# Cross attention of a decoder layer: pieces in the middle of a chunk, a ring of four banks for maxima and pieces, three single banks for scores

## The reference

```python
x = x + retention(layernorm(x))                    # 16 heads of 16, group norm over the batch entry
x = x + cross_attention(layernorm(x), ctx)         # ctx: 8 x 1601 x 256
x = x + mixture_of_experts(layernorm(x))           # 8 experts, 2 chosen, plus a shared one
```

```python
q, k, v = x @ Wq.T + bq, ctx @ Wk.T + bk, ctx @ Wv.T + bv
attn = softmax(q @ k.T / 4)                        # 512 queries x 1601 keys
out = (attn @ v) @ Wo.T + bo
```

## Time and profile before

| what | value |
| --- | --- |
| median of three runs | 2397.34 us |
| the profiled execution | 2399.05 us, of which span 2396.9 |
| PE busy | 2174.8 us (91%) |
| DVE busy | 1511.4 us (63%) |
| ACT busy | 1158.0 us (48%) |
| POOL busy | 431.2 us (18%) |
| first score of cross attention, last one | 464.12, 1957.03 |

### The profile page before, as it was taken

The page is one execution under the profiler, slowest core; times in us unless marked ns, Lnnn a source line. Parts: engine busy times, 40 slices in busy tenths (PEclk is TensorE's granted clock), DMA queues, the critical chain, the costliest instruction groups (busy, mean ns, idle before and its releaser), DMA issues. The chain is left out here.

```text
span 2396.9 us, 35042 instructions
## 1 busy us (share of the span) xinstructions
PE 2174.8 (91%) x12914; PEld 1201.8 (50%) x12946; DVE 1511.4 (63%) x2944; ACT 1158.0 (48%) x1521; POOL 431.2 (18%) x470
## 2 busy tenths in 40 slices
PE   6888867599999999999999999999999978899999
PEld 4656544244444444444444434444443337778887
DVE  6888874476676676676667677667668827622221
ACT  2313121156666666666656666666666663222222
POOL 1101021002102112112111210210211005332222
PEclk9999986589999999999989999999999998999999
DMA  4000005504223321520630531422341001000000
GB/s 160 1 0 0 0 4 100 110 1 100 56 56 82 74 56 50 106 56 2 141 69 1 100 95 16 100 55 56 74 81 29 1 16 59 0 9 9 18 18 18
DMA packets 45360, 118.58 MB, mean 49 GB/s; under 512 B 9120, under 2 KB 21408, under 8 KB 45088
## 3 DMA queue, kind: packets, MB, share of 16 engines
q1 hardware_dynamic: 45232, 116.88, 21.9%
HBM read 77.30 MB, written 38.81 MB: 48 GB/s over the span
## 5 line engine op out<-in xcount | busy, mean ns | idle before, releaser
L1142 DVE TENSOR_REDUCE x_mx<-x_ps 128x1 f32<-128x512 f32 x1536 | 956.1, 684 | 400.8 <-PE x_ps L897 400.1
L1050 ACT ACTIVATE x_probs<-x_ps 128x1024 f32<-128x1024 f32 (+1 forms) x832 | 810.2, 1021 | 507.9 <-PE x_ps L956 507.9
L897 PE MATMUL x_ps<-x_kst,x_qst 48*128 48x512 f32 x1536 | 591.4, 467 | 67.9 <-issue 23.9
L897 PEld LDWEIGHTS x_ps<-x_kst,x_qst 48*128 48x128 f32 x1536 | 264.7, 192 | 583.9 <-DVE x_mx L1142 446.4
L956 PE MATMUL x_ps<-x_qst,x_kst 50*128 50x512 f32 (+1 forms) x1664 | 498.3, 432 | 2.5 <-ACT x_probs L1050 2.4
L944 PE MATMUL x_ps<-x_probs,x_vst 128*17 128x512 f32 (+1 forms) x3328 | 449.1, 612 | 6.3 <-ACT x_ou L1034 5.9
L956 PEld LDWEIGHTS x_ps<-x_qst,x_kst 50*128 50x128 f32 (+1 forms) x1664 | 259.3, 185 | 66.4 <-ACT x_probs L1050 49.9
L1569 DVE TENSOR_TENSOR f_hid_whole<-f_ps,f_act_g 128x512 f32<-128x512 f32 x80 | 55.2, 691 | 241.5 <-PE f_ps L1326 232.9
L1441 ACT ACTIVATE f_act_g<-f_ps 128x512 f32<-128x512 f32 x80 | 47.7, 596 | 246.3 <-remote 126.4
L1507 POOL TENSOR_TENSOR f_hid_rest<-f_hid_whole,f_hid_rounded 128x512 fp32r<-128x512 f32 x80 | 103.1, 1289 | 234.0 <-ACT f_hid_rounded L1447 234.0
L1082 POOL TENSOR_TENSOR x_vst<-x_v_all,x_bv 128x768 f32<-128x768 f32 x64 | 66.4, 1069 | 428.0 <-ACT x_v_all L1009 349.4
(11 more groups left out here) (191 smaller groups left out, 2540.6 us busy)
## 6 DMA issues: line engine op xcount, KB each, us to landing
x_kst<-k_parts SPq DMA_DIRECT2D x192, 200.1 KB, 8.6
k_parts<-x_kp SPq DMA_DIRECT2D x16, 1601.0 KB, 6.1
x_ctxT<-in_ctxT SPq DMA_DIRECT2D x8, 1601.0 KB, 7.4
x_qst<-q_parts SPq DMA_DIRECT2D x192, 64.0 KB, 2.4
q_parts<-x_qp SPq DMA_DIRECT2D x8, 1024.0 KB, 4.3
x_all<-in_x SPq DMA_DIRECT2D x8, 512.0 KB, 3.8
out<-x_all SPq DMA_DIRECT2D x8, 512.0 KB, 2.9
x_qst<-x_mrows SPq DMA_DIRECT2D x128, 4.0 KB
```

What stands on the lines that cost most here:

```text
L897: m = pe.matmul(o, qst[mg][rows, pair, t * P:(t + 1) * P], kst[mg][rows, pair, i * 512:(i + 1) * 512], start=True, stop=True)
L1050: nc.scalar.activation(probs[0:w, s % 4, :, :], ps[0:w, 2 * (s % 2):2 * (s % 2) + 2, :], ACT.Exp, scale=HD ** -0.5).then_inc(exp_done, 1)
L1142: nc.vector.tensor_reduce(out=mx[:, 2 * pair + half, t, i:i + 1], in_=o, axis=AX.X, op=ALU.max).then_inc(drained_v, 1)
```

## The change

Five things are done together, all in cross attention.

- The ring for maxima and pieces has four banks (4 to 7) instead of three; the values' bank is 3.
- Scores have three single banks (0 to 2) instead of two double ones. Heads are counted one by one in the order of issue: score i waits for exponential i-3 and increments `s_filled` itself. ACT runs one exponential of 512 columns per head instead of one of 1024 per pair. `probs` keeps its size.
- The piece of a chunk stands between the two halves: maximum, scores of pair 0, maximum, piece, maximum, scores of pair 1, maximum, values. ACT copies it between the exponentials of pair 0 and those of pair 1, and DVE follows the same order.
- In the prologue the k pieces of f = 1 are split by POOL, after it has placed v of group 0 and before groups 1 to 3.
- In the prologue SP loads the shift rows of group 0 after the spill of f = 1 and before it loads groups 2 and 3.

```diff
-W_BANKS = 3
+W_BANKS = 4
+S_BANKS = 3
-    return [[(first[g][c], second[g][c], pieces[g][c]) for c in range(SC)] for g in range(G)]
+    return [[(first[g][c], pieces[g][c], second[g][c]) for c in range(SC)] for g in range(G)]
-        PV, WORK = 4, 5
+        PV, WORK = S_BANKS, S_BANKS + 1
-        probs = sb("x_probs", [P, 4, 2, T])
+        probs = sb("x_probs", [P, 2 * GH, T])
 # SP
-            for f in range(KT):
-                spill_k(0, f)
-                load_group(0, 2 * f)
-                load_group(0, 2 * f + 1)
+            spill_k(0, 0)
+            load_group(0, 0)
+            load_group(0, 1)
+            spill_k(0, 1)
             load_shift(0, done(LEADER, ("shift", 0)))
+            load_group(0, 2)
+            load_group(0, 3)
 # PE
+            def issued(j):
+                return 2 * (j // 2) + (1 - j % 2)
             def scores(b, g, c, pair):
-                n = b * S_ITEMS + g * 2 * SC + 2 * c + pair
                 w = min(P, S - c * P)
-                if n >= 2:
-                    pe.wait_ge(exp_done, n - 1)
                 for h in (1, 0):
+                    n = GH * (b * CHUNKS + g * SC + c) + issued(2 * pair + h)
+                    if n >= S_BANKS:
+                        pe.wait_ge(exp_done, n - S_BANKS + 1)
                     rows = slice(h * ROWS, h * ROWS + XR + MR)
-                    m = pe.matmul(ps[0:w, 2 * (n % 2) + h, :], kst[g][rows, pair, c * P:c * P + w],
-                                  qst[g][rows, pair, :], start=True, stop=True)
-                m.then_inc(s_filled, 1)
+                    pe.matmul(ps[0:w, n % S_BANKS, :], kst[g][rows, pair, c * P:c * P + w],
+                              qst[g][rows, pair, :], start=True, stop=True).then_inc(s_filled, 1)
...
+                        first, pieces, second = PLANS[b][g][c]
+                        n = woven(b, g, c, 0, n, first)
                         for i in range(len(pieces)):
                             fill(b, n + i, g)
-                        n += len(pieces)
+                        n = woven(b, g, c, 1, n + len(pieces), second)
 # ACT
-                            s = b * S_ITEMS + g * 2 * SC + 2 * c + pair
-                            act.wait_ge(s_filled, s + 1)
-                            if s >= 4:
-                                act.wait_ge(pv_used, s // 2 - 1)
-                            nc.scalar.activation(probs[0:w, s % 4, :, :], ps[0:w, 2 * (s % 2):2 * (s % 2) + 2, :],
-                                                 ACT.Exp, scale=HD ** -0.5).then_inc(exp_done, 1)
+                            x = b * CHUNKS + g * SC + c
+                            for s in range(GH * x + 2 * pair, GH * x + 2 * pair + 2):
+                                act.wait_ge(s_filled, s + 1)
+                                if x >= 2:
+                                    act.wait_ge(pv_used, x - 1)
+                                nc.scalar.activation(probs[0:w, s % (2 * GH), :], ps[0:w, s % S_BANKS, :],
+                                                     ACT.Exp, scale=HD ** -0.5).then_inc(exp_done, 1)
 # POOL
-            for g in range(G):
+            place_v(0)
+            for item in k_pieces(1):
+                split_k(pool, nc.gpsimd, 0, item[1], item[2], done(LEADER, item))
+            for g in range(1, G):
                 place_v(g)
 # DVE, prologue
-                elif item[0] == "k":
+                elif item[0] == "k" and item[1] == 0:
```

More of the change, by code:

```diff
@@ L649 @@
 STARTS = [sum(len(items) for items in ITEMS[:n]) for n in range(len(ITEMS))]
-S_ITEMS = 2 * SC * G
+CHUNKS = SC * G
 LEADER, TRAILER = -1, B
@@ L939, in values, with woven @@
                     pe.wait_ge(v_ready, b * 2 * G + 2 * (g + 1))
-                pe.wait_ge(exp_done, b * S_ITEMS + (g * 2 * SC + 2 * (q + 1)))
+                x = b * CHUNKS + g * SC + q
+                pe.wait_ge(exp_done, GH * (x + 1))
                 w = min(P, S - q * P)
                 for j in range(GH):
-                    slot = (g * 2 * SC + 2 * q + j // 2) % 4
+                    slot = (GH * x + issued(j)) % (2 * GH)
                     m = pe.matmul(ps[32 * j:32 * j + HD + 1, PV, :], vst[g][0:w, q, j, :],
-                                  probs[0:w, slot, j % 2, :], start=q == 0, stop=q == SC - 1)
+                                  probs[0:w, slot, :], start=q == 0, stop=q == SC - 1)
                 m.then_inc(pv_used, 1)
+            def issued(j):
+                return 2 * (j // 2) + (1 - j % 2)
             def scores(b, g, c, pair):
-                n = b * S_ITEMS + g * 2 * SC + 2 * c + pair
                 w = min(P, S - c * P)
-                if n >= 2:
-                    pe.wait_ge(exp_done, n - 1)
                 for h in (1, 0):
+                    n = GH * (b * CHUNKS + g * SC + c) + issued(2 * pair + h)
+                    if n >= S_BANKS:
+                        pe.wait_ge(exp_done, n - S_BANKS + 1)
                     rows = slice(h * ROWS, h * ROWS + XR + MR)
-                    m = pe.matmul(ps[0:w, 2 * (n % 2) + h, :], kst[g][rows, pair, c * P:c * P + w],
-                                  qst[g][rows, pair, :], start=True, stop=True)
-                m.then_inc(s_filled, 1)
+                    pe.matmul(ps[0:w, n % S_BANKS, :], kst[g][rows, pair, c * P:c * P + w],
+                              qst[g][rows, pair, :], start=True, stop=True).then_inc(s_filled, 1)
+            def woven(b, g, c, pair, n, some):
+                ahead = len(some) - 1 if some and all(item[0] == "max" for item in some) else 0
+                for i in range(ahead):
+                    fill(b, n + i, g)
+                scores(b, g, c, pair)
+                for i in range(ahead, len(some)):
+                    fill(b, n + i, g)
+                return n + len(some)
             for n in range(len(PROLOGUE)):
@@ L967, in _ @@
                     for c in range(SC):
-                        *woven, pieces = PLANS[b][g][c]
-                        for pair in range(2):
-                            some = woven[pair]
-                            ahead = len(some) - 1 if some and all(item[0] == "max" for item in some) else 0
-                            for i in range(ahead):
-                                fill(b, n + i, g)
-                            scores(b, g, c, pair)
-                            for i in range(ahead, len(some)):
-                                fill(b, n + i, g)
-                            n += len(some)
+                        first, pieces, second = PLANS[b][g][c]
+                        n = woven(b, g, c, 0, n, first)
                         for i in range(len(pieces)):
                             fill(b, n + i, g)
-                        n += len(pieces)
+                        n = woven(b, g, c, 1, n + len(pieces), second)
                         if c:
@@ L1060, in _ @@
                                 evacuate(b * G + g)
-                        for item in [item for part in PLANS[b][g][c] for item in part]:
-                            if item[0] in BY_ACT:
-                                drain(b, n, g)
-                            n += 1
+                            for item in [item for part in PLANS[b][g][c][2 * pair:2 * pair + 2] for item in part]:
+                                if item[0] in BY_ACT:
+                                    drain(b, n, g)
+                                n += 1
             act.wait_ge(drained_v, done(B - 1, ("norm", G - 2)))
@@ L1102, in _ @@
                 if b:
-                    pool.wait_ge(pv_used, b * (S_ITEMS // 2))
+                    pool.wait_ge(pv_used, b * CHUNKS)
                     place_v(G - 1)
```

4 lines of the change are left out of this document (2 added, 2 removed).

## The result

The changed kernel takes 2212.57 us (median of four, 2199.31 to 2222.89) against 2405.89 of the kernel before in the same comparison (2396.11 to 2418.30): a ratio of 0.9191, 95% interval 0.9111 to 0.9271. The forecast, 2245 of 2397.34, was a ratio of 0.936; so the kernel became faster, by about a quarter more than forecast. The profiled execution took 2199.31 (span 2197.5), 199.7 less than the profiled one of before; the forecast for that difference was 152.

The account below looks back on a forecast made before the run. PE and DVE waiting for each other by turns, from too short a ring, were taken as the bound. Savings of 118 + 7 - 7 + 34 = 152 us from 2399 gave 2247, as median 2245 us; range 2195 to 2310.

Parts of the forecast that it names:

- The ring and the place: Chunks with maxima and a piece: four banks, piece in the middle, 3.93 to 3.56 us, 118 us over 319 chunks.
- the switch from pairs to a full-array matmul: On PE, before piece and before values: 0.42 us from start to start; the middle position's two added switches cost 0.30.
- One saving for all pieces: All 319 chunks with maxima and a piece save 0.37 us each, as the piece's length cancels: 118 us.
- none is late: In chunks with the piece in the middle, DVE drains each bank before PE's next maximum or piece needs it.
- The three score banks: Chunks without a piece: fourth score waits for first exponential, period 2.59; 72 chunks save 7 us, last 17 lose 7.
- Exponentials and increments at nothing: Cross attention: exponentials of 512 at 0.50 us each, covered by PE, and 832 more score increments, both priced at 0.
- The prologue: Start of cross attention: POOL's splits and earlier shift rows bring the first score from 464 to 435; start saves 34 us.
- B: Rival: exponentials' round trip replaces the bank wait even with the piece in the middle; period 3.75, about 2312 us; chance 0.12.
- C: Rival: PE's switches cost nothing where weights load ahead; chunk 3.26 us, whole kernel about 2150 us; chance 0.10.
- A: The forecast itself: chunk with a piece 3.56 us, whole kernel 2245 us; chance 0.64.
- D: Rival: another wait stands behind the first, so only the start counts; 2363 to 2385 us; chance 0.08.
- E: Rival: PE's clock falls in 97 chunks without a piece, adding 176 us; about 2421 us, slower; chance 0.06.

Follow-up runs that it names:

- the transposes chunk above: A transposes chunk of the kernel before with only the piece moved to the middle: chunk 3.29 us; that kernel 2277.16 us, ratio 0.947.
- The experiment at the end: The changed kernel with a fourth score bank, one of the ring's, in the last 17 chunks: 2193.42 us, ratio 0.9121.
- the first profile: The first profiled execution of the changed kernel, with nothing further changed: 2199.31 us; a later profiled execution of the same kernel took 2223.96.
- after: The changed kernel, all five parts against the kernel before: 2212.57 us, ratio 0.9191; run once more, 2211.64 us, ratio 0.9185.

## Why the prediction was right, and where its size was off

**The ring and the place: right, and mis-sized.** PE waited for banks, DVE idled while PE did piece and values, and with the piece in the middle no matmul of a full chunk waits: that is what the timeline shows. The term that was mis-sized is the switch from pairs to a full-array matmul. I priced it at 0.42 from the earlier trace rows and used it twice. Measured, the piece starts 0.32 to 0.33 after the second pair and the values 0.33 after the fourth: 0.34 + 0.33 + 1.06 + 0.34 + 0.33 + 0.98 = 3.38. The maximum of the earlier trace rows was no neutral witness: it had just restarted after a wait and ran 0.49, where one in a flow of pairs runs 0.39. The experiments have both: 0.43 after the delayed fourth pair with the piece at the end, 0.43 after the delayed fourth maximum in the transposes chunk above, 0.33 where the pair before flowed. So a stall costs its own length and another 0.1 behind it. A chunk with a full piece saves 0.54 instead of 0.37, which is outside my own bounds of 0.25 to 0.45; over 319 pieces that is 54 us, and 152 + 54 = 206 is near the measured 199.7. By kinds the saving is 0.54 to 0.56 in most, 0.51 with shift rows, 0.46 in the output projection's second chunk and 0.37 in the second chunk of a group, which has other maxima; those take some of the 54 back, and the clock's low stretches differ by a few us.

**One saving for all pieces: right in sum, not in cause.** I let the length of the piece cancel and counted place and fourth bank as one. They split: place alone gives full pieces all they get, the norm chunk 0.24 and transposes 0.17, and takes 0.08 from the shift rows. The fourth bank gives transposes and shift rows the rest, and the norm chunk 0.11 of its other 0.31. That short chunks then saved about as much as long ones (0.51 to 0.55 against 0.54) is a coincidence of these lengths, and a piece of luck for one price over all 319. Without the fourth bank the kernel stays at 0.9485. That "none is late" holds with three banks too where the piece is full; where it is short, with four only.

**The three score banks: right.** The last chunks take 2.59 to the digit. They lost 11.4 us over 16 lengths (7 forecast), of which near 8 go with the three banks; the forecast started from the 36.8 of the earlier trace rows, a window that holds 2 us of the chunk ahead. The experiment at the end shows that 7.7 could be had back by a fourth bank. Chunks without a piece take 2.63 (2.59 forecast, 2.69 before); with a ring of three they stay at 2.69, so that saving belongs to the fourth bank too.

**Exponentials and increments at nothing: right in the chunks**, each alone. The whole kernel gave 1.006 and 1.0026, both a little above 1 by their intervals, and where the first one's 14 us lie is not shown beyond the lower clock of three executions. The exponential is 0.597 and its pitch 0.49 (four in 2.06), in the bounds.

**The prologue: right.** 31.2 to the first exponential, 4.1 more by the end of group 0: 35 against 34, or 36 with the group's five pieces. Both places where I saw it tight were real: PE waited 4 us for the context, and the low clock lasted into the first chunks. The first was worth little, as loading it earlier showed.

**The rivals.** B's mechanism exists, but not with a piece in the middle: it makes the 3.69 of the piece at the end, and the 2.63 and 2.59 of chunks without one. C (3.26 in a chunk, 0.12 under the measured 3.38) was nearer there than A (3.56, 0.18 over), and further off in the whole kernel (2150, against 2245 and a measured 2212.57): the switches cost, only less. D fell with the first chunk. E forecast a low clock for chunks in which PE waits for an exponential. In batches a low stretch is seen only at a batch's start, where three of the first four chunks have no piece, and not more often than before: in one of the six instead of three. In the last chunks it is seen in some executions: 41 us of the clock at half, and 58 with the piece at the end. That is its kind of loss, 8.5 us against the first profile, a twentieth of its 176, where such chunks stand in a row. Why the clock falls in one execution of the same program and not in another is open; no run here tells it.

**The range.** The chances of what lies outside it add up to 0.30 (C 0.10, D 0.08, E 0.06, half of B 0.06), and not to "some 2 in 10". My bounds on the gaining side (25 us in the chunks, 6 at the start) end at 2214, just above the measured 2212.57, while the range went down to 2195: that it held rests on room that no term had earned. And the low clock of the earlier trace rows lies in the sixth to ninth of the forty slices, not where the prediction's first lines put it.

What stays open besides: the 4.5 us after cross attention, where nothing was edited, and why low clock at the start of batches comes more often with a ring of three (in 3 to 5 of batches 1 to 6 over the six profiles with such a ring, in 0 to 2 over the seven with a ring of four). I saw both and tested neither.

## What to carry to other kernels

When two engines wait for each other by turns, look for a long independent operation and put it between the two halves of what the slower one drains; then ask which operation in that place is too short to cover, since that one needs the extra bank. A price read from a trace belongs to the state around it: take the start-to-start time of a switch where the operation before it flowed, if the changed order will flow. And where a stage lacks the work for which the banks were divided, divide them anew for that stage.

## What the runs showed of the hardware that was not expected

- The first full-array matmul after a pair in different rows starts 0.33 after it when the pair flowed, and 0.43 when the pair had just been held up. The pair held up also shows 0.50 instead of 0.39.
- With 1.2 GHz granted, the last chunks of after had PE's matmuls stand 1.22, 0.79 and 1.91 long in a cycle of 4.04, with one idle stretch of 0.26, and the clock stayed low for 41 us, and for 58 us in another kernel. In the first profile the same chunks kept the high level but for 6.8 us.
- 832 further increments, in matmuls that run at the same time in different rows, left the usual chunks at their 3.92 and 2.69 us.
